# Two attention and feed-forward stacks: the exchange of rotated halves is issued first in SyncE's slot, and waits for the exchange in front of it

## What is computed

```python
for i in range(DEPTH):                       # 6 layers
    x = attn_layer(shift_tokens(x), Wqkv[i], q_scale[i], k_scale[i], Wo[i]) + x
    x = ffn_layer(shift_tokens(x), ln_g[i], ln_b[i], W1[i], b1[i], W2[i], b2[i]) + x
...
q = l2norm(q) * qs                           # 16 heads of 64, k likewise
q = q * cos * scale + rotate_half(q) * sin * scale
k = k * cos * inv + rotate_half(k) * sin * inv
out = local_attention(q, k, v)               # windows of 32: the own and the one in front
```

## The kernel before

| engine | slot j, in this order |
|---|---|
| TensorE (PE) | query projection of unit j (L930); broadcast of inverse norms for unit j-2 (L939, L942); key projection of j (L949); scores of j-2 (L968); **values of unit j-4 (L899)**; value projection of j (L982); output projection of j-4 (L996); a step of the feed-forward |
| VectorE (DVE) | the split of inverse norms (L1225 or L1235, even slots); y += attention of unit j-5 (L1231); normed q and k of unit j-2 (L1257, L1259); rotary products of unit j: cos part into `prc`, sin part into `prs` (L1211, L1213), first q, later k; softmax sums of j-3 (L1273, L1276); maxima of j-2 (L1281) |
| GpSimd (POOL) | probabilities of unit j-3 scaled (L835); **`prc` += `sws` for unit j-1** (L841) |
| SyncE (SP) | all the transfers below |

## Time and profile before

### The profile page before, as it was taken

One profiled execution on the slowest core, in us unless ns is written; L12 is line 12 of the kernel. 1 busy time (PEld: TensorE's weight loads), 2 busy tenths in 40 slices (PEclk: granted clock), 3 DMA queues, 4 the chain that ended last, 5 costly groups with the idle time before them and its releaser, 6 DMA issues. The chain is left out here.

```text
span 4372.0 us, 111762 instructions
## 1 busy us (share of the span) xinstructions
PE 4078.6 (93%) x43089; PEld 2415.8 (55%) x43089; DVE 3362.0 (77%) x4981; ACT 3109.2 (71%) x7032; POOL 1797.4 (41%) x1071
## 2 busy tenths in 40 slices
PE   7997999999999999999967589999999999999998
PEld 3443555555555555555536545555555555555554
DVE  5774888888888888888735478888888888888885
ACT  3555777777777777777762267777777777777776
POOL 3112444444444444444404534444444444444442
PEclk7997999999999999999986599999999999999999
DMA  2212444444443444444300044444444444444342
GB/s 43 31 21 72 96 110 101 106 95 103 104 104 93 112 103 96 106 98 104 80 10 3 3 111 107 103 94 106 108 96 109 99 105 96 103 103 107 93 100 49
DMA packets 232516, 380.70 MB, mean 87 GB/s; under 512 B 59365, under 2 KB 122337, under 8 KB 231689
## 3 DMA queue, kind: packets, MB, share of 16 engines
q1 hardware_dynamic: 231560, 372.20, 36.7%
q10 hardware_dynamic: 384, 0.79, 0.1%
HBM read 39.22 MB, written 1.05 MB: 9 GB/s over the span
## 5 line engine op out<-in xcount | busy, mean ns | idle before, releaser
L835 POOL TENSOR_TENSOR b_prob<-b_prob,b_rinv 128x768 f32<-128x768 f32 x384 | 564.2, 1469 | 1797.0 <-DVE b_rinv L1276 1797.0
L841 POOL TENSOR_TENSOR b_prc<-b_prc,b_sws 128x1024 f32<-128x1024 f32 x384 | 906.7, 2361 | 70.8 <-DMA b_sws<-b_prs 70.6
L1138 ACT ACTIVATE b_prob<-ps,b_nmx 128x96 f32<-128x96 f32 x3072 | 748.9, 362 | 0.0
L1211 DVE SCALAR_TENSOR_TENSOR b_prc<-ps,b_qks,b_rot 128x512 f32<-128x512 f32 x768 | 570.6, 743 | 11.8 <-ACT b_sq L1099 11.5
L1213 DVE SCALAR_TENSOR_TENSOR b_prs<-ps,b_qks,b_rot 128x512 f32<-128x512 f32 x768 | 569.5, 742 | 0.0
L1257 DVE TENSOR_TENSOR b_prc<-b_prc,ps 128x512 f32<-128x512 f32 x384 | 263.5, 686 | 384.9 <-PE ps L942 305.4
L1074 ACT ACTIVATE b_pT<-ps 128x512 f32<-128x512 f32 x724 | 434.8, 601 | 129.8 <-PE ps L879 127.9
L879 PEld LDWEIGHTS ps<-ident,b_prob 128*128 128x128 f32 x3072 | 381.5, 141 | 219.8 <-ACT b_pT L1074 121.3
L879 PE MATMUL ps<-ident,b_prob 128*128 128x128 f32 x3072 | 461.4, 273 | 5.9 <-ACT b_pT L1074 5.8
L982 PE MATMUL ps<-b_wqkv,b_xs 128*128 128x256 f32 x1536 | 434.1, 405 | 2.2 <-DVE b_prs L1213 2.2
L1119 ACT ACTIVATE b_oT<-ps 128x512 f32<-128x512 f32 x384 | 226.8, 591 | 293.7 <-PE ps L899 293.7
(11 more groups left out here) (293 smaller groups left out, 7294.5 us busy)
## 6 DMA issues: line engine op xcount, KB each, us to landing
b_sws<-b_prs SPq DMA_DIRECT2D x1536, 128.0 KB
b_vs<-b_va SPq DMA_DIRECT2D x384, 256.0 KB, 3.8
b_wqkv<-in_L_ffn_Wqkv SPq DMA_DIRECT2D x96, 192.0 KB, 3.5
b_xs<-y SPq DMA_DIRECT2D x126, 128.0 KB, 2.3
b_wo<-in_L_ffn_Wo SPq DMA_DIRECT2D x96, 64.0 KB, 3.2
b_xs<-y SPq DMA_DIRECT2D x42, 127.8 KB, 2.3
b_rot<-in_rot SPq DMA_DIRECT2D x2, 2048.0 KB, 7.9
b_w<-in_L_ffn_W SPq DMA_DIRECT2D x24, 170.5 KB
```

Source lines behind the costliest of these rows:

```text
L835: pool.tensor_tensor(prob[:, r, :, P - KEYS:P], prob[:, r, :, P - KEYS:P], rinv[:, r % 2, :].rearrange("p (b a) -> p b a", a=1).broadcast_ ...
L841: pool.tensor_tensor(prc[:, r, :, :], prc[:, r, :, :], sws[:, r % 2, :, :], ALU.add)\
L1138: g = act.activation(prob[:, kb, i, P - KEYS:P], wide[0][:, e * CH + m * KEYS:e * CH + (m + 1) * KEYS], ACT.Exp, bias=nmx[:, kb % 2, i:i + 1])
L1211: dve.scalar_tensor_tensor(out=prc[:, r, i, :], in0=bank[i][:, :], scalar=scale, in1=rot[:, 2 * i, t], op0=ALU.mult, op1=ALU.mult)
```

## The change

In SyncE's slot the exchange of unit a = unit(0) moves from near the end to a place behind the shifted copy of y and ahead of the value transfers, the loads of `wqkv` and `wo` and the feed-forward's weights. It still waits for `pk_done` of its own unit. Its second wait was for the addition of unit b = unit(1), one unit in front, and is now for the landing of that unit's exchange.

```diff
                     if e and closes(e) and not ending(e):
                         ...
+                    if a:
+                        U, r = um(a)
+                        sp.wait_ge(S["pk_done"], ONE + U + 1)
+                        if b:
+                            sp.wait_ge(S["swap_ld"], ONE + 64 * (um(b)[0] + 1))
+                        for h in range(4):
+                            o = h ^ 1
+                            sp.dma_start(sws[32 * o:32 * o + 32, r % 2, :, :], prs[32 * h:32 * h + 32, r % 2, :, :])\
+                                .then_inc(S["swap_ld"], 16)
                     if b:
                         U, r = um(b)
                         if r % 2:
                             ...
-                    if a:
-                        U, r = um(a)
-                        sp.wait_ge(S["pk_done"], ONE + U + 1)
-                        if b:
-                            sp.wait_ge(S["add_done"], ONE + um(b)[0] + 1)
-                        for h in range(4):
-                            o = h ^ 1
-                            sp.dma_start(sws[32 * o:32 * o + 32, r % 2, :, :], prs[32 * h:32 * h + 32, r % 2, :, :])\
-                                .then_inc(S["swap_ld"], 16)
```

## The result

| | before | changed |
|---|---|---|
| median, four executions each | 4369.6 us | 4607.03 us |
| lowest to highest | 4368.14 to 4377.39 | 4588.86 to 4612.65 |
| ratio to before, 95% interval | | 1.0533 [1.0505, 1.0561] |
| profiled execution | 4373.69 | 4588.86 (span 4587.2) |

The changed kernel is 5.3% slower. The forecast was 4512 us with 4440 to 4570 as its range, so the sign and the main mechanism were right, the size too small, and one wait was missing. The profiled execution is the fastest of the four. It shows 4588.86 - 4373.69 = 215 us of the 237 us; its mean granted clock is 0.948, that of the other three 0.922 to 0.945.

A forecast was written before the change was run, and what follows sets the result against it. TensorE, 98% busy in the stacks, was taken to bound the kernel. The profiled 4373.7 us, less 6 saved, plus 104.6 of late values and 40 of lowered clock, gave 4512.3; the forecast was 4512 us, range 4440 to 4570.

The forecast's parts named there:

- That TensorE is the bound and everything it waits for counts: In the stacks TensorE is 98% busy, so anything that makes it wait adds to the time nearly in full.
- The saving of 6 us: GpSimd's addition waits 22.8 us for the exchange in the stacks; an earlier exchange was taken to save 6 of them.
- The chain of 7.15 us: From `pk_done` through SyncE's wake-up, four exchange issues and two value transfers to `vs` landed: 7.15 us.
- stops of kinds 4 and 12: Slots with j mod 16 of 4 or 12: values late by 0.70 and 0.35 us, 22 times each, 15.4 + 7.7 us.
- stops of kind 8: Slots with j mod 16 of 8: values late by 2.75 us, counted in full 22 times, 60.5 us.
- stops of kind 0 less slack: Slots with j mod 16 of 0: values late by 1.95 us, less 1.2 us slack, 28 times, 21.0 us.
- nobody waits: In SyncE's queue, the `wqkv` and `wo` loads stand up to 4 us later, many slots ahead of use, at no cost.
- term of the clock: TensorE's 50 longer stops: 15 and 9 falls to half clock at 1.7 us each, 40 us, bounds 0 to 85.
- row of before that held its clock over 2.8 us: In the kernel before, full clock stayed after 2.8 us without a matmul; evidence that stops this long can go either way.
- rival in which the clock falls at nearly every stop: TensorE's clock falls at nearly every stop, or for longer than 3.4 us: 4555 to 4600 us, chance 0.08.
- size of the stops: TensorE's waits for late values over 94 slots: 104.6 us, or 138 us with no slack anywhere.
- rival of a delay that is mostly absorbed: TensorE's pauses elsewhere, 12 us in each 600, take up most of the delay: 4415 to 4425 us, chance 0.1.

The follow-up runs named there:

- variant with slots 4g+2 alone: The changed kernel with the exchange ahead of the value transfers only in slots 4g+2, behind them elsewhere: 4395.38 us, 1.0048 of the kernel before.
- filled kernels: The changed kernel plus two unused matmuls ahead of the wait for values in slots 9 and 25, or also 1 and 17: 4561.12 and 4547.19 us.

## Why the prediction was right and where it failed

**That TensorE is the bound and everything it waits for counts:** right. Steps of units without a stop did not change (by 1.3 us at most in the sum of one kind), but for those of units 2 modulo 16, which wait for the copy of `y`.

**The saving of 6 us:** right, as far as the runs can tell. The waits less what L1225 gives back leave 6.6 us, the steps of units 2 modulo 16 are 6.3 us shorter and all steps of the stacks 2.3 us, and the ratios are 0.9985 and 0.9987. The Trainium skill, page "SBUF — State Buffer", section "Who interferes with whom", states that a VectorE instruction with two SBUF inputs and a GpSimd instruction that reads SBUF contend. This agrees: with the exchange on time 36 instead of 25 of the 38 L1225 took over 2 us.

**The chain of 7.15 us:** right. Values started 7.17 to 7.34 us behind `pk_done` in five of the eight kinds of slot that j modulo 32 gives (medians), and 7.5 to 8.0 in the others, 0, 16 and 24. In the five the parts agree: some 2.65 us to the first value transfer, 4.5 to 4.65 us from there to landing.

**The terms**, forecast against the profiled execution:

| term | forecast | measured |
|---|---|---|
| stops of kinds 4 and 12 | 15.4 + 7.7 = 23.1 | 22.0 + 13.3 = 35.3 |
| stops of kind 8 | 60.5 | 75.8 |
| stops of kind 0 less slack | 21.0 | 55.9 - 22 x 1.3 = 27.3 |
| clock | 40 | (114.2 - 75.8) + (53.7 - 27.3) = 64.8 |
| units 2 modulo 16: saving and copy of `y` | -6 | 21.3 |
| sum | 138.6 | 224.5 |

The 1.3 us of slack are the median stop less the median growth at the 7 slots of kind 0 where the clock held, 2.10 - 0.78; the forecast had 1.2. Of the 86 us between the two sums the stops make 34, the copy of `y` 27 and the clock 25.

**The step that failed first is "nobody waits"** in the part on the other moves. I looked at weights, and at the value transfers themselves, but not at the transfer that stands behind the value transfers of slots 4g+2 in the queue: the copy of `y` in the slot after. It makes 21.3 + 6 = 27 us of the difference, shown apart by the variant with slots 4g+2 alone (29 us).

**The second is the term of the clock**, 40 us, which measures 65. It is the count that failed, 24 falls for 37. I gave the long stops two falls in three and the short ones one in three; 22 of 24 fell, and 15 of 22. The cost of one was right: 64.8 / 37 = 1.75 us against 1.7. That is in part luck, since I took each fall as 3.4 us at half clock, ten of the 38 pieces lasted 6.8 us, and part of many lay in the stop itself or in slack. The row of before that held its clock over 2.8 us was a poor guide: it lay outside the stacks, and in them none of the 27 stops of 2.7 us and more held. The filled kernels show this term causally: 60 us came back. The rival in which the clock falls at nearly every stop had a chance of 0.08 with 4555 to 4600 us, where the profiled execution lies (the median of 4607 us is above it). That its number fits is in part luck: it adds 105 us of stops and 85 of clock, and measured are 138, 65 and 27 for a copy that it does not have.

**The third, and the largest, is the size of the stops**, 138 us with no slack in the forecast, 172 us measured. Part of it is the count. I took the first half layer of a stack as kind 0 throughout, and its slots behave as their own kinds. Kind 8 then has 24 slots rather than 22, kinds 4 and 12 have 24 each, and kind 0 has 22 rather than 28. The other part is the landing in slots 24 of a layer, and in slots 16 of the first stack, 5.3 to 6.3 us in many where it is 4.5 to 4.6 in most of the rest. Its cause stays open.

**What stays open:** why those landings are slow (the loads right behind them explain some 0.6 us in slots 16, and nothing in slots 24 by the medians), and 22 us between what the profiled executions show (215 us) and the medians (237 us). The three others of the changed kernel had a lower mean clock, so more or longer falls are likely, in the stacks or outside them, where the clock was at half for 290 to 376 us over the twelve profiled kernels; they have no trace. The rival of a delay that is mostly absorbed is out: in kinds 4, 8 and 12 the steps grew by nearly the whole stop or more.

## What to carry to other kernels

When a transfer with a late wait is moved ahead in a queue that runs in order, write down every transfer behind it up to the next such wait, in this slot and the next, with the slot in which each is needed: it is the transfer that is used soonest, not the one that is moved, that sets the price. Here the gain of some 6 us could be had without the move, by waiting for the right thing (the landing instead of the addition) where the exchange stood.

A stop of nearly 3 us on a dense TensorE should be priced at nearly twice its length (kind 8: stops of 2.80 us, steps longer by 5.07, medians), since the clock falls with it. Where a stop can't be avoided, unused matmuls in it can pay, as they did here; where there was none, the same matmuls cost 34 us.

## What the runs showed of the hardware

- Inside a dense stretch of TensorE, idle times of 2.7 to 4.5 us brought the granted clock to half (1.2 GHz) in 21 of 21 cases, those of 1.9 to 2.7 us in 17 of 26, shorter ones in none of 47. It stayed there for 3.4 or 6.8 us, though work was at hand again once the values had landed. With unused matmuls in the stops there were 25 and 10 pieces instead of 38.
- An issue of a 128 to 256 KB transfer holds SyncE's queue for about 0.6 us (2.42 us for four, 0.65 us for one), and this time, four times over, was the greater part of the delay.
- Two value transfers of the same size landed 4.5 to 4.6 us behind the first's issue in most slots and up to 6.3 us in some, in slots 16 in all six layers of the first stack (5.06 to 6.29 us) and in none of the second (4.60 to 4.65). With the loads behind them moved by a slot these six were some 0.6 us faster; for the rest no reason was found.
- VectorE's L1225, which reads two operands from SBUF, took 0.74 us alone and some 2.33 us beside GpSimd's addition; 36 of 38 did so when the exchange was on time, 25 before.
